# A graph network kernel on one core: round 0's gathered rows go through TensorE into PSUM before VectorE takes their maxima

## The chip, the cores and the metric

One Trainium2 chip, one of its cores. The metric is the time of one execution on the device in microseconds (us). The kernel before was run three times. Beside those runs stands one profiled execution, from which all rows here come.

## The reference, cut to what matters

There are 6250 nodes with 256 features each, and 100000 edges, sorted by their destination `dst`; `src` is random. All arithmetic is float32.

```python
# layer 0 (round 0 of the kernel)
theta_x = (x[dst] - x[src]) @ theta_w.T + theta_b
e = relu(theta_x + x[src] @ phi_w.T + phi_b)
x = layernorm(x + segment_max(e, dst))
# layer 1 (rounds 1 and 2)
hv = x @ W_in + b_in
for W, b in ((W_u0, b_u0), (W_u1, b_u1)):
    m = relu(concat([hv[src], edge_attr_64]) @ W + b)
    hv = where(has_in, segment_max(m, dst) + hv, hv)
x = layernorm(x + relu(hv @ W_ro + b_ro))
```

The part of an edge's message that hangs on the destination alone is the same for all edges of a run, so it can be added after the maximum. What is left per edge is a row of a table, picked by `src` (and in rounds 1 and 2 a product of the edge's 64 attributes).

## The kernel before, in words

Each of three rounds does the same four things. First a product over all nodes makes a table in HBM, `table0` to `table2` (49 tiles of 128 nodes, handled in 25 units of two). Then the edge pass goes over all edges. Its slots are laid out as 128 partitions of 784 steps, so a partition holds 784 edges in order of `dst`, and a step handles one edge of each partition. Then runs that cross from one partition to the next are joined, and at last the maxima are gathered back by node, which feeds the next round's products.

The edge pass is where most of the time lies. Its 784 steps are 49 turns of 16 steps (`BODY`). Four engines work on it side by side, each with its own written order, held together by semaphores:

- GpSimd (`gather_edges`, L518 to L527) issues one indirect DMA per step. It brings 128 rows of 256 floats from the table, by the indices in `src_sb`, into the ring `gath` of G = 36 slots in SBUF. Every second step it waits until the slot's old rows have been used.
- TensorE, in rounds 1 and 2 (`messages`, L732 to L749), sums two steps at a time in a PSUM bank of `edge_ps`: the product of the edge attributes (L744), then the gathered rows, multiplied by the identity (L746). Six banks are used in turn (`EDGE_BANKS`), so TensorE may be 12 steps ahead of VectorE.
- VectorE (`edge_maxima`, L342 to L366) makes one running maximum per step (L356): `hist[s] = max(hist[s-1] + lift[t], edges)`, where `lift` is very negative at the start of a run. In rounds 1 and 2 `edges` comes from PSUM; in round 0 it is the gathered row in SBUF itself, and VectorE waits for the gather's semaphore directly.
- SyncE stores each 8 steps of `hist` to `runs` in HBM (L472).

Round 0 has more to do beside this. For each turn there is a query: VectorE makes a one-hot matrix in the middle of the turn (`pick_rows`, L279 and L281), TensorE multiplies it by `dst_f` into `query_ps`, banks 4 and 5 of `edge_ps` (`pick`, L693), and after the turn VectorE counts in it where the runs of 128 nodes end (`find_ends`, L286 to L298). TensorE also makes one base product of a tile of nodes per turn (`back`, L685 and L687), which ScalarE copies out of `back_ps` (L595). Once, after turn 1, it multiplies the weights of layer 1 with one another (`multiply_weights`, L725 and L729). Its inputs need `bias_columns` on VectorE (L315). VectorE takes the results in `weights_and_biases` (L321 to L338) after turn 2. In round 0 TensorE's order is therefore: base products, query, weight products, turn by turn, with no matmul of edges among them (L769 to L774).

GpSimd in round 0 waits for `state_done`, which VectorE raises every two steps; in rounds 1 and 2 for `group_summed`, which TensorE raises every two steps (L521 to L524).

Of the kernel before, what the change touches and what calls it, by code (L numbers as in the profile page):

```python
# [5 lines left out]
P = 128  # L6
# [14 lines left out]
HE_CHUNKS = STEPS // HC  # L21
NHE = 4
BANKS = 4
EDGE_BANKS = 6
TILES = -(-NODES // P)
NPAD = TILES * P

# [6 lines left out]
XT_BUFS, ROW_BUFS, UNIT_BUFS = 12, 8, 4  # L34
CONV, NEXT0, NEXT1, OUT = range(4)
LATE_TURN = 1
FIRST_X_CHUNK = 20
assert TURNS == TILES and STEPS % SC == 0 and H % SC == 0 and G % GS == 0 and STEPS % HC == 0 and HC % GS == 0 and SC % GS == 0


def gnn_kernel(nc, a):
# [13 lines left out]
    with ctx:  # L55
# [76 lines left out]
        staged = lambda u: slots(hist, 2 * UNIT_BUFS, UNIT_BUFS, u)  # L132
        assert 2 * XT_BUFS <= G and 2 * (ROW_BUFS + UNIT_BUFS) <= G and 4 * UNIT_BUFS <= H

        edge_ps = ctx.enter_context(nc.psum_tensor("edge_ps", [P, EDGE_BANKS, 2 * D], f32))
        side_ps = ctx.enter_context(nc.psum_tensor("side_ps", [P, 2, 2 * D], f32))
        wide = lambda u: (unit(u)[1] - unit(u)[0]) * D
        product_ps = lambda u: edge_ps[:, u % BANKS, 0:wide(u)]
        turned_ps = lambda u: edge_ps[:, BANKS + u % 4, 0:wide(u)] if u % 4 < 2 else side_ps[:, u % 4 - 2, 0:wide(u)]
        query_ps = edge_ps[:, BANKS:BANKS + 2, :].rearrange("p b f -> p (b f)")  # L140
        back_ps = side_ps[:, 0, 0:D]
        join_ps = [edge_ps[:, BANKS + n, 0:D] for n in range(2)]

        cleared = sem("cleared")
# [90 lines left out]
        def _(dve):  # L235
# [81 lines left out]

            def weights_and_biases():
                dve.wait_ge(weights_mult, 1)
                for n, w in enumerate((w_in_n0, w_in_n1, w_in_ro)):  # L320
                    V.tensor_copy(flat(w[:, :, :]), edge_ps[:, n, :])  # L321
                for n, b_ps in ((NEXT0, edge_ps[:, 3, 0:D]), (NEXT1, edge_ps[:, 3, D:]), (OUT, side_ps[:, 1, 0:D])):
                    V.tensor_tensor(b_full[:, n, :], b_ps, rest[:, n, :], ALU.add)
                V.tensor_tensor(b_full[:, CONV, :], rest[:, CONV, :], b_add, ALU.add)
                after()
                V.tensor_copy(part[0], b_full)
                after()
                V.tensor_tensor(rest, b_full, part[0], ALU.subtract)
                after()
                V.tensor_copy(part[1], rest)  # L330
                after()
                V.tensor_tensor(rest, rest, part[1], ALU.subtract)
                after()
                V.tensor_copy(part[2], rest)
                V.tensor_scalar(b_parts[:, :, :], part[0], row_is[:, 0:1], None, ALU.mult)
                for m in (1, 2):
                    after()
                    last = V.scalar_tensor_tensor(b_parts[:, :, :], part[m], row_is[:, m:m + 1], b_parts[:, :, :],  # L338
                                                  ALU.mult, ALU.add)
                reached("all", last)  # L340

            def edge_maxima(r):  # L342
                for t in range(STEPS):
                    s = r * STEPS + t
                    if r == 0 and t % BODY == BODY // 2:
                        pick_rows(col_no[:, :])
                    if s % SC == 0 and s >= H:
                        dve.wait_ge(stored[s // SC % NS], 16 * (s // H))
                    if r == 0 and s % 2 == 0:
                        dve.wait_ge(gathered[s % G // 2], 2 * 16 * (s // G + 1))  # L350
                    elif r > 0 and s % GS == 0:
                        dve.wait_ge(group_summed, s // GS - GROUPS + 1)
                    V.drain()
                    bank, half = s // 2 % EDGE_BANKS, s % 2 * D
                    edges = gath[:, s % G, :] if r == 0 else edge_ps[:, bank, half:half + D]
                    state = V.scalar_tensor_tensor(hist[:, s % H, :], hist[:, (s - 1) % H, :], lift[:, t:t + 1], edges,  # L356
                                                   ALU.add, ALU.max)
                    if s % GS == GS - 1:
                        state.then_inc(state_done, 1)
                    if r == 0 and t % BODY == BODY - 1:  # L360
                        i = t // BODY
                        find_ends(i + 1, node_no[:, 0:1], end_row[:, i:i + 1], float(P))
                        if i == LATE_TURN:
                            bias_columns()
                        if i == LATE_TURN + 1:
                            weights_and_biases()  # L366

            def join_runs(r):
                dve.wait_ge(fix_turned, r + 1)
# [137 lines left out]
        def _(pool):  # L507
# [10 lines left out]
            def gather_edges(r):  # L518
                for t in range(STEPS):
                    s = r * STEPS + t  # L520
                    if s % GS == 0 and G <= s < STEPS + G:  # L521
                        pool.wait_ge(state_done, (s - G) // GS + 1)
                    elif s % GS == 0 and s >= G:
                        pool.wait_ge(group_summed, (s - G) // GS - GROUPS + 1)  # L524
                    pool.indirect_dma_start(gath[:, s % G, :], None, tables[r],  # L525
                                            bass.IndirectOffsetOnAxis(src_sb[:, t:t + 1], 0)
                                            ).then_inc(gathered[s % G // 2], 16)  # L527
# [41 lines left out]
        def _(act):  # L569
# [8 lines left out]
            def load_he(r, c):  # L578
                n = (r - 1) * HE_CHUNKS + c
                if n >= NHE:  # L580
                    act.wait_ge(group_summed, (n - NHE + 1) * HC // GS)
                act.dma_start(he_sb[:, n % NHE, :], a["he"][:, c * HC // 2 * P:(c + 1) * HC // 2 * P]
                              ).then_inc(he_loaded[n % NHE], 16)

# [94 lines left out]
        def _(pe):  # L679
# [39 lines left out]
            def multiply_weights():  # L719
                pe.wait_ge(setup_step, setup_at["b_in columns"])  # L720
                rights = (w_n0, w_n1, w_ro)
                for n, w in enumerate(rights):
                    for m in range(KH):
                        for h in range(KH):
                            T.matmul(edge_ps[:, n, m * D:(m + 1) * D], w_inT[:, h, m * P:(m + 1) * P], w[:, h, :],  # L725
                                     start=(h == 0), stop=(h == KH - 1))
                for w, to in zip(rights, (edge_ps[:, 3, 0:D], edge_ps[:, 3, D:], side_ps[:, 1, 0:D])):
                    for h in range(KH):
                        last = T.matmul(to, b_in_cols[:, h, :], w[:, h, :], start=(h == 0), stop=(h == KH - 1))  # L729
                last.then_inc(weights_mult, 1)  # L730

            def messages(r):  # L732
                for g in range(GROUPS):
                    n = (r - 1) * GROUPS + g
                    c = n * GS // HC
                    if n * GS % HC == 0:
                        pe.wait_ge(he_loaded[c % NHE], 16 * (c // NHE + 1))
                    if g * GS >= 2 * EDGE_BANKS:
                        pe.wait_ge(state_done, r * GROUPS + g - 2 * EDGE_BANKS // GS + 1)
                    for k in range(0, GS, 2):  # L740
                        s = r * STEPS + g * GS + k
                        bank = edge_ps[:, s // 2 % EDGE_BANKS, :]
                        at = s % HC // 2 * P
                        T.matmul(bank, he_sb[:, c % NHE, at:at + P], w_e[r - 1][:, :], start=True, stop=False)  # L744
                        pe.wait_ge(gathered[s % G // 2], 2 * 16 * (s // G + 1))
# [20 lines left out]

            for r in range(ROUNDS):
                if r == 0:
                    for i in range(TURNS):  # L769
                        for t in back_tiles(0, i):  # L770
                            back(t)
                        pick(i + 1)
                        if i == LATE_TURN:
                            multiply_weights()  # L774
                else:
                    pe.wait_ge(product_out, (r + 1) * NU)
                    messages(r)
# [62 lines left out]
```

## Time and profile before

| | us |
|---|---|
| median of three runs | 3344.41 (3342.88 to 3352.03) |
| the profiled execution's own time | 3344.26 |
| its span, first to last instruction | 3342.5 |

| engine | busy us | share of the span |
|---|---|---|
| TensorE matmul (PE) | 2113.1 | 63% |
| VectorE (DVE) | 1462.9 | 44% |
| ScalarE (ACT) | 188.2 | 6% |
| GpSimd (POOL) | 2412.3 | 72% |

The busy time of an engine is the sum of its instructions. It does not say what the engine waited for; the chain of waits and the groups of instructions by line do. Round 0's gathers start at 56.9 us, round 1's at 1190.5 us and round 2's at 2259.1 us. PE, PEld, DVE, ACT, POOL and SP are the profile's names of TensorE's matmul, its weight load, VectorE, ScalarE, GpSimd and SyncE. L12 is line 12 of the kernel. A float32 matmul shows as two records.

### The profile page before, as it was taken

Reading aid. Unit: us, or ns where it says so; the run is one execution under the profiler, and the core shown is the slowest. Engines: PE = TensorE matmul, PEld = TensorE weight load, DVE = VectorE, ACT = ScalarE, POOL = GpSimd, SP = SyncE. Lnnn points to the kernel's source line nnn. Section 1 sums busy time; section 2 is a strip of 40 time slices with the busy share of each in tenths; the row PEclk is TensorE's granted clock in tenths of the full one; section 3 lists DMA queues with packets and bytes.
Section 4 is the critical chain, followed back from the end, with each engine's and each line's share of the span. In section 5 each row is a group of like instructions: output and inputs, shape, how many; then the busy total and the mean of one; then the engine's idle time right before and its main releaser. Section 6 shows DMA issues by size and latency. Waiting matters only on the chain.

```text
span 3342.5 us, 21987 instructions
## 1 busy us (share of the span) xinstructions
PE 2113.1 (63%) x5442; PEld 1057.8 (32%) x5442; DVE 1462.9 (44%) x3430; ACT 188.2 (6%) x422; POOL 2412.3 (72%) x2536
## 2 busy tenths in 40 slices
PE   5322222222222678788888887877888888888877
PEld 4211111111111433333333333353443433333335
DVE  2655555555555523333433333423333333333337
ACT  1000000000000510000000000010000000000005
POOL 4777777777776457777777777757777777777766
PEclk8655555555555999999999999988999999999989
DMA  7666666666665557777777776776777777777765
GB/s 251 209 214 221 222 223 227 224 225 215 211 218 187 183 190 238 248 243 237 249 239 245 245 240 237 247 249 215 255 248 260 245 243 249 253 255 251 244 207 151
DMA packets 265662, 770.03 MB, mean 230 GB/s; under 512 B 55444, under 2 KB 114687, under 8 KB 227903
## 3 DMA queue, kind: packets, MB, share of 16 engines
q0 software_dynamic: 122208, 334.92, 32.9%
q1 hardware_dynamic: 84478, 354.64, 28.1%
q10 hardware_dynamic: 58848, 79.06, 8.0%
q8 instruction: 44, 0.72, 0.1%
q14 instruction: 84, 0.68, 0.1%
HBM read 421.22 MB, written 347.19 MB: 230 GB/s over the span
## 4 chain that ended last, share of the span: by engine, by line
POOL 46%; DMA 17%; issue 16%; PE 16%; DVE 3%; ACT 2%; DVEq 0%; ACTq 0%; POOLq 0%
POOL gath L525 45%; DMA gath<-table,src_sb 15%; PE edge_ps L746 6%; PE edge_ps L744 3%; PE edge_ps L685 3%; PE side_ps L685 2%; DVE hist L356 1%; POOL gath L552 1%; ACT x_sb L636 1%; DVE hist L393 1%; DMA gath<-runs,end_row 0%; ACT gath L636 0%; DMA runs<-hist 0%; PE edge_ps L757 0%; PE side_ps L757 0%
## 5 line engine op out<-in xcount | busy, mean ns | idle before, releaser
L525 POOL DMA_INDIRECT gath<-table,src_sb x2352 | 2244.7, 954 | 788.9 <-issue 670.3
L356 DVE SCALAR_TENSOR_TENSOR hist<-hist,lift,edge_ps 128x256 f32<-128x256 f32 x1568 | 752.6, 480 | 1231.4 <-PE edge_ps L746 1169.9
L746 PE MATMUL edge_ps<-gath,ident 128*128 128x512 f32 x1568 | 860.7, 632 | 335.7 <-DMA gath<-table,src_sb 334.8
L744 PE MATMUL edge_ps<-w_e,he_sb 128*128 128x512 f32 x1568 | 820.0, 605 | 1.0 <-DVE hist L416 0.5
L693 PE MATMUL edge_ps<-dst_f,onehot 128*128 128x512 f32 x200 | 145.9, 883 | 731.7 <-DVE onehot L281 731.7
L356 DVE SCALAR_TENSOR_TENSOR hist<-hist,lift,gath 128x256 f32<-128x256 f32 x784 | 380.9, 486 | 426.8 <-DMA gath<-table,src_sb 382.8
L746 PEld LDWEIGHTS edge_ps<-gath,ident 128*128 128x128 f32 x1568 | 288.2, 196 | 799.4 <-DMA gath<-table,src_sb 540.4
L744 PEld LDWEIGHTS edge_ps<-w_e,he_sb 128*128 128x128 f32 x1568 | 298.4, 196 | 351.0 <-issue 335.1
L693 PEld LDWEIGHTS edge_ps<-dst_f,onehot 128*128 128x128 f32 x200 | 57.8, 318 | 811.1 <-DVE onehot L281 760.5
L595 ACT COPY hv_sb<-side_ps 128x256 f32<-128x256 f32 x147 | 54.7, 372 | 2886.0 <-PE edge_ps L746 1867.5
L552 POOL DMA_INDIRECT gath<-runs,end_row x147 | 147.7, 1005 | 65.9 <-issue 40.2
L685 PE MATMUL side_ps<-w_theta,back_T 128*128 128x256 f32 x196 | 83.9, 575 | 21.0 <-DVE b_parts L338 19.3
L685 PEld LDWEIGHTS side_ps<-w_theta,back_T 128*128 128x128 f32 x196 | 60.6, 311 | 41.2 <-DVE b_parts L338 19.8
L685 PE MATMUL side_ps<-w_in_n,back_T 128*128 128x256 f32 x196 | 69.7, 493 | 0.0
L685 PE MATMUL side_ps<-w_in_ro,back_T 128*128 128x256 f32 x196 | 65.3, 467 | 0.0
L685 PEld LDWEIGHTS side_ps<-w_in_n,back_T 128*128 128x128 f32 x196 | 48.9, 249 | 36.4 <-issue 31.1
L685 PEld LDWEIGHTS side_ps<-w_in_ro,back_T 128*128 128x128 f32 x196 | 47.6, 243 | 37.1 <-issue 32.1
L685 PE MATMUL side_ps<-w_ro,back_T 128*128 128x256 f32 x196 | 58.2, 425 | 0.0
L685 PE MATMUL edge_ps<-w_ro,hist 128*128 128x256 f32 x196 | 50.4, 401 | 11.2 <-ACT hist L623 11.2
L289 DVE TENSOR_SCALAR_CACHE_REDUCE junk<-edge_ps,node_no 128x784 f32<-128x784 f32 x49 | 50.6, 1033 | 4.8 <-issue 0.4
L685 PE MATMUL edge_ps<-w_in_n,hist 128*128 128x256 f32 x196 | 50.7, 389 | 0.0
L286 DVE TENSOR_SCALAR_CACHE_REDUCE junk<-edge_ps,node_no 128x784 f32<-128x784 f32 x49 | 50.3, 1027 | 0.0
(125 smaller groups left out, 906.9 us busy)
## 6 DMA issues: line engine op xcount, KB each, us to landing
runs<-hist SPq DMA_DIRECT2D x294, 1024.0 KB, 5.2
he_sb<-in_he ACTq DMA_DIRECT2D x196, 256.0 KB, 2.9
gath<-table,src_sb POOLq DMA_INDIRECT x2352, 3.3
table<-hist SPq DMA_DIRECT2D x72, 256.0 KB, 2.8
back_T<-x1T ACTq DMA_DIRECT2D x98, 128.0 KB, 3.2
back_T<-in_xT ACTq DMA_DIRECT2D x49, 128.0 KB, 2.5
x_sb<-in_x SPq DMA_DIRECT2D x49, 128.0 KB, 4.8
back_T<-msgT ACTq DMA_DIRECT2D x49, 128.0 KB, 5.9
```

The lines of the kernel that those rows point to most:

```text
L286: V.tensor_scalar(junk[:, :], query_ps[:, 0:STEPS], nodes, 0.0, ALU.is_le, ALU.add, accum_out=counts[:, 0:1])
L289: V.tensor_scalar(junk[:, :], query_ps[:, 0:STEPS], nodes, 0.0, ALU.is_lt, ALU.add, accum_out=counts[:, 1:2])
L356: state = V.scalar_tensor_tensor(hist[:, s % H, :], hist[:, (s - 1) % H, :], lift[:, t:t + 1], edges, ALU.add, ALU.max)
L393: V.scalar_tensor_tensor(y, y, 0.0, flat(x_sb[:, lo:hi, :]), ALU.max, ALU.add)
L525: pool.indirect_dma_start(gath[:, s % G, :], None, tables[r], bass.IndirectOffsetOnAxis(src_sb[:, t:t + 1], 0)).then_inc(gathered[s % G // ...
L552: pool.indirect_dma_start(rows(u)[:, k, :], None, runs[0:SPARE, :], bass.IndirectOffsetOnAxis(end_row[:, lo + k:lo + k + 1], 0)).then_inc( ...
L595: A.copy(hv_sb[:, n % TILES, :], back_ps).then_inc(back_kept, 1)
L636: last = A.activation(to[:, k, :], of[:, k, :], ACT.Identity, bias=shift[:, at, k:k + 1], scale=rstd[:, at, k:k + 1])
L685: last = T.matmul(to, left, right, start=(m == 0), stop=(bias is None and m == len(terms) - 1))
L693: last = T.matmul(query_ps[:, lo:hi], onehot[:, :], dst_f[:, lo:hi], start=True, stop=True)
L744: T.matmul(bank, he_sb[:, c % NHE, at:at + P], w_e[r - 1][:, :], start=True, stop=False)
L746: last = T.matmul(bank, ident[:, :], flat(gath[:, s % G:s % G + 2, :]), start=False, stop=True)
```

## The change

In round 0 TensorE now multiplies each pair of gathered steps by the identity into a PSUM bank (`first_rows`), and VectorE's L356 takes `edges` from that bank, as in the other rounds. VectorE waits for `group_summed` in all rounds, and so does GpSimd. Round 0 uses three banks in turn, since banks 4 and 5 hold the query. The base products, the query and the weight products stand inside `first_rows`, between the pairs: base products after the third pair of a turn, the query for the turn after its seventh pair, the weight products after the second pair of turn 2. Their results go to banks 3 to 5 and the side banks instead of banks 0 to 3, and VectorE takes them at step 40, the middle of turn 2, ahead of that turn's `pick_rows`. The other edits follow the new counts of `group_summed`.

```diff
-EDGE_BANKS = 6
+EDGE_BANKS = (3, 6, 6)
+WEIGHTS_AT = (LATE_TURN + 1) * BODY + BODY // 2
...
+        weights_ps = [edge_ps[:, BANKS, :], edge_ps[:, BANKS + 1, :], side_ps[:, 0, :]]
+        edge_bank = lambda r, t: edge_ps[:, t // 2 % EDGE_BANKS[r], :]
...
             def edge_maxima(r):
                 for t in range(STEPS):
                     s = r * STEPS + t
+                    if r == 0 and t == WEIGHTS_AT:
+                        weights_and_biases()
                     if r == 0 and t % BODY == BODY // 2:
                         pick_rows(col_no[:, :])
...
-                    if r == 0 and s % 2 == 0:
-                        dve.wait_ge(gathered[s % G // 2], 2 * 16 * (s // G + 1))
-                    elif r > 0 and s % GS == 0:
-                        dve.wait_ge(group_summed, s // GS - GROUPS + 1)
+                    if s % GS == 0:
+                        dve.wait_ge(group_summed, s // GS + 1)
                     V.drain()
-                    bank, half = s // 2 % EDGE_BANKS, s % 2 * D
-                    edges = gath[:, s % G, :] if r == 0 else edge_ps[:, bank, half:half + D]
+                    edges = edge_bank(r, t)[:, t % 2 * D:(t % 2 + 1) * D]
...
-                    if s % GS == 0 and G <= s < STEPS + G:
-                        pool.wait_ge(state_done, (s - G) // GS + 1)
-                    elif s % GS == 0 and s >= G:
-                        pool.wait_ge(group_summed, (s - G) // GS - GROUPS + 1)
+                    if s % GS == 0 and s >= G:
+                        pool.wait_ge(group_summed, (s - G) // GS + 1)
...
+            def first_rows():
+                for g in range(GROUPS):
+                    turn_no, at = g // (BODY // GS), g % (BODY // GS) * GS
+                    if g == 0:
+                        pe.wait_ge(product_out, NU)
+                    if g * GS >= 2 * EDGE_BANKS[0]:
+                        pe.wait_ge(state_done, g - 2 * EDGE_BANKS[0] // GS + 1)
+                    for t in range(g * GS, (g + 1) * GS, 2):
+                        pe.wait_ge(gathered[t % G // 2], 2 * 16 * (t // G + 1))
+                        last = T.matmul(edge_bank(0, t), ident[:, :], flat(gath[:, t % G:t % G + 2, :]),
+                                        start=True, stop=True)
+                    last.then_inc(group_summed, 1)
+                    if turn_no == LATE_TURN + 1 and at == BODY // 8:
+                        multiply_weights()
+                    if at == BODY // 4:
+                        for t in back_tiles(0, turn_no):
+                            back(t)
+                    if at == BODY - 2 * GS:
+                        pick(turn_no + 1)
...
             for r in range(ROUNDS):
                 if r == 0:
-                    for i in range(TURNS):
-                        for t in back_tiles(0, i):
-                            back(t)
-                        pick(i + 1)
-                        if i == LATE_TURN:
-                            multiply_weights()
+                    first_rows()
```

## Rows read from the trace of the kernel before

**Rows 1.** Chain of waits: shares of the span by engine and line.

```profile
POOL gath L525 45%; DMA gath<-table,src_sb 15%; PE edge_ps L746 6%; PE edge_ps L744 3%; PE edge_ps L685 3%; PE side_ps L685 2%; DVE hist L356 1%; POOL gath L552 1%; ACT x_sb L636 1%; DVE hist L393 1%; DMA gath<-runs,end_row 0%; ACT gath L636 0%; DMA runs<-hist 0%; PE edge_ps L757 0%; PE side_ps L757 0%
```

**Rows 2.** Groups of instructions (count, busy us, mean ns, idle before): L525, rounds 0, 1.

```profile
L525 POOL DMA_INDIRECT gath<-table,src_sb x784 | 762.2, 972 | 261.9 <-issue 227.3 <-DMA table<-hist 23.3 <-DVE hist L356 11.3
...
L525 POOL DMA_INDIRECT gath<-table,src_sb x784 | 741.3, 946 | 278.0 <-issue 220.6 <-DMA table<-hist 39.4 <-PE edge_ps L746 16.8
```

**Rows 3.** Line L525: ns min/median/max, first and last start, rounds 0, 1, 2.

```profile
L525 POOL DMA_INDIRECT gath<-table,src_sb x784: 942/946/1761, 56.9 to 1056.7; - x196
...
L525 POOL DMA_INDIRECT gath<-table,src_sb x784: 942/946/962, 1190.5 to 2169.5; - x196
...
L525 POOL DMA_INDIRECT gath<-table,src_sb x784: 942/946/957, 2259.1 to 3237.8; - x196
```

**Rows 4.** Groups of instructions: L356 in round 0 and in round 1.

```profile
L356 DVE SCALAR_TENSOR_TENSOR hist<-hist,lift,gath 128x256 f32<-128x256 f32 x782 | 380.0, 486 | 425.6 <-DMA gath<-table,src_sb 381.6 <-issue 0.9
...
L356 DVE SCALAR_TENSOR_TENSOR hist<-hist,lift,edge_ps 128x256 f32<-128x256 f32 x778 | 373.5, 480 | 616.4 <-PE edge_ps L746 585.8 <-issue 1.7
```

**Rows 5.** Timeline (start us, duration us, instruction, idle before): gathers and VectorE, rounds 0, 1.

```profile
66.78 1.62 DVE L356 SCALAR_TENSOR_TENSOR hist<-hist,lift,gath 128x256 f32<-128x256 f32 x3 [8.89 <-DMA gath<-table,src_sb]
66.94 1.14 POOL L525 DMA_INDIRECT gath<-table,src_sb  x1 [0.30 <-issue]
...
127.73 1.23 DVE L328 TENSOR_TENSOR x_sb<-x_sb 128x1024 f32<-128x1024 f32 x1
128.19 1.66 POOL L525 DMA_INDIRECT gath<-table,src_sb  x1 [0.30 <-issue]
...
1052.90 1.04 POOL L525 DMA_INDIRECT gath<-table,src_sb  x1 [0.30 <-issue]
...
1204.90 1.04 DVE L356 SCALAR_TENSOR_TENSOR hist<-hist,lift,edge_ps 128x256 f32<-128x256 f32 x2 [1.66 <-PE edge_ps L746]
...
1205.50 0.95 POOL L525 DMA_INDIRECT gath<-table,src_sb  x1 [0.31 <-issue]
```

**Rows 6.** Busy by stretch (length, busy us of each engine, granted clock, DMA): in round 0.

```profile
690.00:890.00 200.00, 43.28 (x82) 23.98 (x83) 110.20 (x278) 3.52 (x10) 152.04 (x157) 0.54 0.66 215
```

**Rows 7.** Timeline: TensorE at the lower clock, rounds 0 and 1.

```profile
72.55 2.99 PE L693 MATMUL edge_ps<-dst_f,onehot 128*128 128x512 f32 x4 [18.63 <-DVE onehot L281]
...
157.12 1.91 PE L685 MATMUL side_ps<-w_theta,back_T 128*128 128x256 f32 x4
...
1194.52 2.07 PE L746 MATMUL edge_ps<-gath,ident 128*128 128x512 f32 x2 [6.00 <-DMA gath<-table,src_sb]
...
1198.09 1.91 PE L746 MATMUL edge_ps<-gath,ident 128*128 128x512 f32 x2
...
1199.80 1.45 PE L744 MATMUL edge_ps<-w_e,he_sb 128*128 128x512 f32 x2
```

**Rows 8.** Timeline: weight products, the query behind them, VectorE's block.

```profile
104.27 3.78 PE L725 MATMUL edge_ps<-x_sb 128*128 128x256 f32 x8 [10.00 <-DVE x_sb L315]
...
114.15 1.48 PE L693 MATMUL edge_ps<-dst_f,onehot 128*128 128x512 f32 x4
...
120.73 1.03 DVE L286 TENSOR_SCALAR_CACHE_REDUCE junk<-edge_ps,node_no 128x784 f32<-128x784 f32 x1
...
123.67 1.28 DVE L321 COPY w_in_n<-edge_ps 128x512 f32<-128x512 f32 x2
...
132.26 2.65 DVE L338 SCALAR_TENSOR_TENSOR b_parts<-x_sb,row_is,b_parts 128x1024 bf16<-128x1024 bf16 x2
```

**Rows 9.** Timeline: the end of the edge pass, rounds 0 and 1.

```profile
1056.74 0.95 POOL L525 DMA_INDIRECT gath<-table,src_sb  x1 [0.30 <-issue]
...
1059.52 1.04 DVE L356 SCALAR_TENSOR_TENSOR hist<-hist,lift,gath 128x256 f32<-128x256 f32 x2 [1.19 <-DMA gath<-table,src_sb]
...
2174.13 1.13 PE L746 MATMUL edge_ps<-gath,ident 128*128 128x512 f32 x2 [0.77 <-DMA gath<-table,src_sb]
...
2175.36 1.03 DVE L356 SCALAR_TENSOR_TENSOR hist<-hist,lift,edge_ps 128x256 f32<-128x256 f32 x2 [1.72 <-PE edge_ps L746]
```

More of the change, by code:

```diff
@@ L133, in gnn_kernel @@
         assert 2 * XT_BUFS <= G and 2 * (ROW_BUFS + UNIT_BUFS) <= G and 4 * UNIT_BUFS <= H
-        edge_ps = ctx.enter_context(nc.psum_tensor("edge_ps", [P, EDGE_BANKS, 2 * D], f32))
+        edge_ps = ctx.enter_context(nc.psum_tensor("edge_ps", [P, max(EDGE_BANKS), 2 * D], f32))
         side_ps = ctx.enter_context(nc.psum_tensor("side_ps", [P, 2, 2 * D], f32))
@@ L319, in weights_and_biases @@
                 dve.wait_ge(weights_mult, 1)
-                for n, w in enumerate((w_in_n0, w_in_n1, w_in_ro)):
-                    V.tensor_copy(flat(w[:, :, :]), edge_ps[:, n, :])
+                for w, w_ps in zip((w_in_n0, w_in_n1, w_in_ro), weights_ps):
+                    V.tensor_copy(flat(w[:, :, :]), w_ps)
                 for n, b_ps in ((NEXT0, edge_ps[:, 3, 0:D]), (NEXT1, edge_ps[:, 3, D:]), (OUT, side_ps[:, 1, 0:D])):
@@ L364, in edge_maxima @@
                             bias_columns()
-                        if i == LATE_TURN + 1:
-                            weights_and_biases()
             def join_runs(r):
@@ L580, in load_he @@
                 if n >= NHE:
-                    act.wait_ge(group_summed, (n - NHE + 1) * HC // GS)
+                    act.wait_ge(group_summed, GROUPS + (n - NHE + 1) * HC // GS)
                 act.dma_start(he_sb[:, n % NHE, :], a["he"][:, c * HC // 2 * P:(c + 1) * HC // 2 * P]
@@ L724, in multiply_weights @@
                         for h in range(KH):
-                            T.matmul(edge_ps[:, n, m * D:(m + 1) * D], w_inT[:, h, m * P:(m + 1) * P], w[:, h, :],
+                            T.matmul(weights_ps[n][:, m * D:(m + 1) * D], w_inT[:, h, m * P:(m + 1) * P], w[:, h, :],
                                      start=(h == 0), stop=(h == KH - 1))
@@ L737, in messages @@
                         pe.wait_ge(he_loaded[c % NHE], 16 * (c // NHE + 1))
[L738 to L742, printed above, removed]
+                    if g * GS >= 2 * EDGE_BANKS[r]:
+                        pe.wait_ge(state_done, r * GROUPS + g - 2 * EDGE_BANKS[r] // GS + 1)
+                    for t in range(g * GS, (g + 1) * GS, 2):
+                        s = r * STEPS + t
+                        bank = edge_bank(r, t)
                         at = s % HC // 2 * P
```

## The prediction, made before the changed kernel ran

> **What bounds the kernel now.** I read the chain of waits first. The gather that GpSimd issues, L525, has 45% of it alone, and its transfers another 15% [rows 1]. Then I read the groups of instructions, one round at a time [rows 2]. In each round GpSimd issues 784 gathers. Between two of them it stands 0.30 us of "issue"; nothing else holds it inside a round: the 11.3 us put down to VectorE in round 0 are 37 of those same 0.30 us steps, and the 23.3 us are the wait for the table before the first gather. So each round lasts 784 times (one gather plus 0.30), whatever TensorE and VectorE do, as long as they keep up. They do: VectorE is idle 425.6 us in round 0, nearly all of it waiting for gathered rows [rows 4], and TensorE is busy 43 us of 200 [rows 6].
>
> The reader should see one oddity. The same gather takes 972 ns on average in round 0 and 946 ns in round 1 [rows 2], with a longest of 1761 against 962 ns [rows 3]. From first to last start, round 0 needs 1056.7 - 56.9 = 999.8 us and round 1 needs 2169.5 - 1190.5 = 979.0 us [rows 3]: 20.8 us more for the same 784 gathers (busy alone: 762.2 - 741.3 = 20.9 [rows 2]).
>
> **Where the 20.9 us come from.** I went to the timeline of round 0. 143 of 784 gathers take over 0.97 us; the first that meets an L356 starts at 66.94, the last at 1052.90 [rows 5]. Their pattern is sharp. At 66.78 VectorE begins an L356; at 0.48 us each it ends at 67.26. At 66.94 a gather starts, and takes 1.14 us instead of 0.95, so 0.19 longer. 67.26 is 0.32 after its start. Going through all of them, a gather is stretched when a VectorE instruction with two SBUF tensors as inputs is already running and lasts beyond about 0.14 us after the gather's start; the stretch is what it lasts beyond that (0.32 - 0.14 = 0.18). The longest fits too: L328, two SBUF inputs, runs from 127.73 to 128.96; the gather of 128.19 takes 1.66, so 0.71 more, and 128.96 - (128.19 + 0.14) = 0.63 [rows 5]. In round 1 L356 takes one input from PSUM, and still meets gathers: from 1204.90 a pair of L356 runs for 1.04 us, to 1205.94, and the gather that starts under the second of them, at 1205.50, takes 0.95 [rows 5]. No gather of rounds 1 and 2 takes more than 962 ns [rows 3]. So it is the second SBUF input, not VectorE's writes or its being busy. Going by which instruction lay over each gather's start, L356 carries 18.6 us of the 20.9, L328 and L332 together 1.5, and the small ones (L281's two-input comparison above all) and noise the rest.
>
> The Trainium skill (SBUF — State Buffer, on engine ports and the shared port pair) says a VectorE instruction with two SBUF inputs contends with a GpSimd instruction that reads SBUF, and that the later one waits until the other ends; the trace agrees, since the stretch ends with the VectorE instruction, and a gather reads its indices from SBUF. The same page infers that a two-input operation takes only the read interface while descriptor generation needs the write interface, which would leave a DMA issue untouched. By that sentence the gain of this change would be nil (a rival below); the 143 stretched gathers speak against it here.
>
> **The change part by part**, against the profiled execution's 3344.3 us (span 3342.5, and 1.8 around it); the median of the three runs is 3344.4, so the sums carry over.
>
> (1) Round 0's L356 reads its edge operand from PSUM. It becomes the L356 of rounds 1 and 2, 480 ns for 486 [rows 4]; VectorE's own time doesn't count, it is hidden by its 425.6 us of idling. What counts is the 18.6 us of stretched gathers: -18.6. Bounds: -20.9 if all stretch goes, 0 if round 1's lack of stretch had another reason. I take -18.6, as rounds 1 and 2 show the new form with none.
>
> (2) TensorE gets 392 new identity matmuls of 128x512, two gathered rows each. Each shows as two records; such a pair takes 2.07 us at the lower clock when it comes after a pause, and 1.71 from start to start when work follows work (1198.09 to 1199.80) [rows 7]. Per turn of 16 gathers (20.0 us of GpSimd): 8 x 1.71 = 13.7, a query 2.99, a base product 1.91, together 18.6 us even at the lower clock [rows 7]; at the higher one about half (a query 1.48 [rows 8], an identity pair 1.13 alone [rows 9]). That fits into 20.0, and the gather ring holds 36 rows, 45 us. Cost while it fits: 0. If it did not: the rival below.
>
> (3) Queries now wait in TensorE's order behind the matmul of steps 12 and 13 of a turn, and VectorE asks at step 8, so the query is ready when TensorE comes to it; VectorE needs the answer after step 15. TensorE's 2.99 us fall between two pairs due 2.5 us apart, so VectorE may run 1 to 2 us late at a turn's end and make it up: it needs 16 x 0.56 (a pair 1.04 less one 0.48 [rows 5]) and the search for run ends, 2.9 us (120.73 to 123.67 [rows 8]), of a turn's 20. GpSimd is now released by TensorE, not VectorE, and never has been close to the release. Cost 0; bounds 0 to 1 us, at the last turn alone.
>
> (4) The weight products (TensorE from 104.27 to 114.15 us) now stand ahead of round 0's matmuls, and VectorE's block that takes them (123.67 to 134.9) starts at step 40 instead of after 47 [rows 8]. While they run, TensorE sums nothing: it holds at step 36 for 10 us, then gets at most three pairs ahead of VectorE and holds at step 46 while VectorE works its 11 us block. At about 130 us GpSimd has issued (130 - 57)/1.25 = 58 gathers and may issue 46 + 36 = 82: 24 gathers, 30 us, are left. VectorE recovers 5 us per turn. Cost 0; if the ring didn't cover it, at most 10 + 11 = 21 us. L328 and L332 stay, with two SBUF inputs, and can again meet two gathers (1.5 us, kept in the sum) or none. The base products are two per turn in turns 3 to 5, 1.9 us each more, also inside the reserve.
>
> (5) Edge banks 3 instead of 6 in round 0: TensorE is at most 6 steps ahead, 7.5 us of gathers, against VectorE's 2.9 us search at a turn's end. Cost 0. The counts in GpSimd's and ScalarE's waits only follow the new numbering; rounds 1 and 2 wait for the same events: 0.
>
> (6) The end of round 0. Now the last gather starts at 1056.74 and VectorE takes its rows at 1059.52, 2.8 us later [rows 9]. A matmul comes between landing and VectorE: in round 1 it starts at 2174.13 and VectorE follows at 2175.36, 1.2 us [rows 9]; at the lower clock 2.07 and the 0.1 us step to VectorE, 2.2 [rows 7]. All of it is on the path. I take +1.7, between the two, because TensorE's clock in this stretch may be either. The queries' chain at the end keeps its distance. At the start of round 0 TensorE is free before the first rows land: 0.
>
> Sum: -18.6 + 1.7 = -16.9; 3344.3 - 16.9 = 3327.4, about 3327 us. Own range: gathers -20.9 to -16 (L281 and the rest may meet more gathers once L356 no longer pushes them), end +1.2 to +2.2 with 2 us either way for how long the last transfers take to land: 3321 to 3333.
>
> **Rivals.**
> (a) The stretch does not go, 6%. Either the gathers are held by VectorE for a reason that PSUM doesn't mend, or TensorE's new reads of the gather ring replace it. Against it: TensorE reads the same ring in rounds 1 and 2 with 946 ns gathers. Then 3344.3 + 1.7 = 3346. (The inference of the Trainium skill's page SBUF — State Buffer, told above, would give this number too.)
> (b) TensorE becomes the bound in round 0 and the kernel is slower, 5%. Its place: each pair released singly at the lower clock, so that 2.07 counts each time instead of 1.71: 8 x 2.07 + 2.99 + 1.91 = 21.5 us per turn against 20.0. From turn 3 on that is 46 x 1.5 = 69 us; the ring hides the 30 us that (4) leaves of it, and the rest, 39, shows: 3327 + 39 = 3366. It decides from 20.0 us per turn on. For it: the granted clock is 0.54 in round 0 [rows 6]. Against it: a late TensorE has its pairs waiting, and then 1.71 holds; and in round 1 the clock rose after 6 us of such work: the pair of 1199.80 takes 1.45 [rows 7].
> (c) Partial: the remaining two-input instructions fall into step with the gathers, or the weight phase costs some of its 21 us, so that 8 to 12 us of the gain go: 3337, 7%.
>
> **How the numbers follow.** Forecast 82%, (a) 6%, (b) 5%, (c) 7%. Range 3321 to 3337: the forecast's own, widened to (c). A change under 0.3%, 10 us, can't be told from none here. Faster (under 3334): 0.87, the forecast and a part of (c); same 0.08; slower 0.05, (b) alone.
>
> **What would show it.** Right: the gathers of round 0 average 946 to 950 ns, and some 980 us lie between first and last start; longest ones only at L328, L332; VectorE released by TensorE; GpSimd idle in steps of 0.30 only; VectorE's last pair some 4.5 us after the last gather's start instead of 2.8. Wrong: gathers still at 972 ns (a); idle of GpSimd released by TensorE in round 0, longer than 0.3 each (b, or the weight phase in c).

## The result, and the profile after

Over eight runs the changed kernel takes 3334.39 us (3332.28 to 3338.73), the kernel before 3344.20 us in as many. The medians lie 9.8 us apart. The ratio is 0.9966 with a 95% interval of 0.9958 to 0.9975, which is 8 to 14 us faster. The prediction said 3327, in a range from 3321 to 3337. The profiled execution took 3333.97 us with a span of 3332.2.

The gather is L523 now and the maximum L358. The chain of waits of the changed kernel still has the gather at its head, with 41% instead of 45% [rows 1]:

```profile
POOL gath L523 41%; DMA gath<-table,src_sb 17%; PE edge_ps L764 6%; PE edge_ps L683 3%; PE edge_ps L739 3%; PE edge_ps L762 3%; PE side_ps L683 3%; POOL gath L550 1%; ACT x_sb L634 1%; PE edge_ps L691 1%; DMA gath<-runs,end_row 1%; DVE hist L393 1%; ACT gath L634 0%; DMA runs<-hist 0%; PE side_ps L775 0%
```

The groups of instructions of round 0 in the changed kernel (count, busy us, mean ns, idle before), gather and maximum:

```profile
L523 POOL DMA_INDIRECT gath<-table,src_sb x784 | 743.1, 948 | 261.5 <-issue 227.6 <-DMA table<-hist 23.0 <-PE edge_ps L739 11.0
...
L358 DVE SCALAR_TENSOR_TENSOR hist<-hist,lift,edge_ps 128x256 f32<-128x256 f32 x782 | 375.3, 480 | 414.6 <-PE edge_ps L739 363.6 <-issue 0.9
```

and the gather's line: ns min/median/max, first and last start in round 0:

```profile
L523 POOL DMA_INDIRECT gath<-table,src_sb x784: 942/946/1763, 56.6 to 1037.3; - x196
```

The gather is down from 972 to 948 ns [rows 2], and first and last start lie 980.7 us apart instead of 999.8 [rows 3]. The 11.0 us that name TensorE are 36 steps of 0.30: GpSimd never waited for a free slot. VectorE is idle 415 us around its maxima, about as long as before [rows 4], now behind TensorE.

Cutting the two spans at GpSimd's instructions gives the whole account (us; "fix" is the read of rows to fix, GpSimd's first instruction after a round's gathers):

| stretch | before | after | difference |
|---|---|---|---|
| to round 0's first gather | 56.9 | 56.6 | -0.3 |
| round 0, first to last gather | 999.9 | 980.7 | -19.1 |
| round 0, last gather to fix | 8.5 | 15.6 | +7.1 |
| fix to round 1's first gather | 125.2 | 125.9 | +0.6 |
| round 1, first to last gather | 979.0 | 978.6 | -0.4 |
| to round 2's first gather | 89.7 | 91.3 | +1.6 |
| round 2, first to last gather | 978.7 | 978.9 | +0.2 |
| to the end | 104.7 | 104.7 | 0.0 |

The gain is there in full, and 7.1 us are given back in a single place, the end of round 0. This is its timeline in the changed kernel:

```profile
1030.14 2.46 ACTq L580 DMA_DIRECT2D he_sb<-in_he  x4
...
1035.21 0.32 SPq L472 DMA_DIRECT2D runs<-hist  x1
...
1037.28 0.95 POOL L523 DMA_INDIRECT gath<-table,src_sb  x1 [0.30 <-issue]
1037.82 2.04 PE L739 MATMUL edge_ps<-gath,ident 128*128 128x512 f32 x2 [0.91 <-DMA gath<-table,src_sb]
...
1040.89 2.04 PE L739 MATMUL edge_ps<-gath,ident 128*128 128x512 f32 x2 [1.03 <-DMA gath<-table,src_sb]
1042.73 2.83 PE L691 MATMUL edge_ps<-dst_f,onehot 128*128 128x512 f32 x4
...
1045.35 1.73 PE L739 MATMUL edge_ps<-gath,ident 128*128 128x512 f32 x2
1047.18 1.04 DVE L358 SCALAR_TENSOR_TENSOR hist<-hist,lift,edge_ps 128x256 f32<-128x256 f32 x2 [3.10 <-PE edge_ps L739]
...
1052.91 0.94 POOL L532 DMA_INDIRECT fix_rows<-runs,fix_from  x1 [14.69 <-DMA runs<-hist]
```

VectorE takes the last pair 9.9 us after the last gather's start, against 2.8 [rows 9]. Two things can be seen. The pair before the last is still waiting for its rows (the releaser is the DMA) 3.6 us after the last gather has started. Then the last turn's query takes 2.6 us ahead of the last pair. The last two pairs of matmuls take 2.04 and 1.73 us, where c0 below has 1.10 for the same work; the granted clock just before them is 0.50 (second view below). There is also something that the prediction did not have: four loads of edge attributes for round 1 (`he_sb`), 256 KB each, 7.1 us before the last gather. In the kernel before they start 20.4 us before it:

```profile
1036.33 1.79 ACTq L582 DMA_DIRECT2D he_sb<-in_he  x4
```

ScalarE issues them after it has copied out the last base product, and that product moved from turn 47 into turn 48. The store of eight steps of maxima that lies nearest to the last gather moved too: it started 6.2 us before it and starts 2.1 us before it now, since VectorE gets to those steps later. The stretches around the last gather (length, busy of each engine, and at the end clock, DMA share, GB/s), before and then after, show what this does: the DMA engines are full where they used to have room.

```profile
1048.70:1052.70 4.00, 1.31 (x2) 0.80 (x3) 2.66 (x8) 0.00 (x0) 2.98 (x4) 0.50 0.59 210
1052.70:1056.70 4.00, 1.68 (x3) 0.38 (x2) 0.96 (x3) 0.00 (x0) 2.92 (x3) 0.50 0.84 262
```

```profile
1029.30:1033.30 4.00, 1.70 (x7) 0.65 (x5) 3.42 (x13) 1.04 (x2) 2.96 (x4) 0.98 0.93 281
1033.30:1037.30 4.00, 2.49 (x3) 0.50 (x2) 2.65 (x7) 0.62 (x1) 2.90 (x4) 0.50 1.06 395
```

### The profile page after: what moved, and what is told of

Read it like the earlier page. It is cut to its first block, busy times and chain, and to the rows that moved or that the text cites. A ratio compares the mean times of both kernels' runs of the same rounds, so it can differ in the third digit from the quotient of the medians.

```text
span 3332.2 us, 23945 instructions
## 1 busy us (share of the span) xinstructions
PE 2514.5 (75%) x6226; PEld 1198.1 (36%) x6226; DVE 1459.7 (44%) x3430; ACT 188.4 (6%) x422; POOL 2394.7 (72%) x2536
## 4 chain that ended last, share of the span: by engine, by line
POOL 43%; PE 19%; DMA 19%; issue 15%; ACT 2%; DVE 2%; DVEq 0%; ACTq 0%; POOLq 0%
POOL gath L523 41%; DMA gath<-table,src_sb 17%; PE edge_ps L764 6%; PE edge_ps L683 3%; PE edge_ps L739 3%; PE edge_ps L762 3%; PE side_ps L683 3%; POOL gath L550 1%; ACT x_sb L634 1%; PE edge_ps L691 1%; DMA gath<-runs,end_row 1%; DVE hist L393 1%; ACT gath L634 0%; DMA runs<-hist 0%; PE side_ps L775 0%
## 5 line engine op out<-in xcount | busy, mean ns | idle before, releaser
L523 POOL DMA_INDIRECT gath<-table,src_sb x2352 | 2225.4, 946 | 789.7 <-issue 667.8
L358 DVE SCALAR_TENSOR_TENSOR hist<-hist,lift,edge_ps 128x256 f32<-128x256 f32 x2352 | 1129.0, 480 | 1649.0 <-PE edge_ps L764 1169.7
L764 PE MATMUL edge_ps<-gath,ident 128*128 128x512 f32 x1568 | 856.4, 629 | 333.3 <-DMA gath<-table,src_sb 332.5
L739 PE MATMUL edge_ps<-gath,ident 128*128 128x512 f32 x784 | 483.1, 732 | 342.2 <-DMA gath<-table,src_sb 324.6
L764 PEld LDWEIGHTS edge_ps<-gath,ident 128*128 128x128 f32 x1568 | 288.6, 195 | 792.8 <-DMA gath<-table,src_sb 530.7
L739 PEld LDWEIGHTS edge_ps<-gath,ident 128*128 128x128 f32 x784 | 155.2, 228 | 599.0 <-issue 341.9
L691 PE MATMUL edge_ps<-dst_f,onehot 128*128 128x512 f32 x200 | 93.7, 600 | 11.1 <-DVE onehot L284 11.1
L691 PEld LDWEIGHTS edge_ps<-dst_f,onehot 128*128 128x128 f32 x200 | 47.0, 236 | 76.3 <-issue 63.2
L683 PE MATMUL side_ps<-w_theta,back_T 128*128 128x256 f32 x196 | 72.8, 511 | 1.7 <-ACT hv_sb L593 1.7
L683 PEld LDWEIGHTS side_ps<-w_theta,back_T 128*128 128x128 f32 x196 | 52.6, 270 | 45.2 <-issue 39.3
L292 DVE TENSOR_SCALAR_CACHE_REDUCE junk<-edge_ps,node_no 128x784 f32<-128x784 f32 x49 | 50.6, 1033 | 4.8 <-issue 0.4
```

The lines of the kernel that those rows point to most:

```text
L292: V.tensor_scalar(junk[:, :], query_ps[:, 0:STEPS], nodes, 0.0, ALU.is_lt, ALU.add, accum_out=counts[:, 1:2])
L683: last = T.matmul(to, left, right, start=(m == 0), stop=(bias is None and m == len(terms) - 1))
L691: last = T.matmul(query_ps[:, lo:hi], onehot[:, :], dst_f[:, lo:hi], start=True, stop=True)
L739: last = T.matmul(edge_bank(0, t), ident[:, :], flat(gath[:, t % G:t % G + 2, :]), start=True, stop=True)
L764: last = T.matmul(bank, ident[:, :], flat(gath[:, s % G:s % G + 2, :]), start=False, stop=True)
```

## The experiments

Two questions were open: whether the second SBUF input alone makes the 19 us, and what costs 7 us at the end of round 0. The runs of each table row were compared with runs of the kernel before on the same chip. "Stream" is first to last gather of round 0, "end" is last gather to fix.

| kernel | stream | end | ratio to before (95%) |
|---|---|---|---|
| before | 999.9 | 8.5 | |
| after | 980.7 | 15.6 | 0.9966 (0.9958 to 0.9975) |
| c0_changed_again | 981.6 | 13.1 | 0.9966 (0.9952 to 0.9979) |
| e1_sbuf_max | 1003.6 | 14.5 | 1.0024 (1.0014 to 1.0033) |
| e2_stale_psum | 981.4 | 8.5 | 0.9950 (0.9936 to 0.9963) |
| e5_one_input | 992.2 | 8.3 | 0.9971 (0.9959 to 0.9982) |
| e3_query_early | 981.6 | 14.5 | 0.9966 (0.9954 to 0.9978) |
| e4_direct_tail | 981.8 | 12.1 | 0.9962 (0.9948 to 0.9975) |
| e8b_all_three | 984.1 | 9.0 | 0.9951 (0.9938 to 0.9965) |
| e9b_before_late_loads | 999.9 | 10.2 | 1.0002 (0.9993 to 1.0011) |

Stream and end are of one profile each. The last two rows ran on a chip where the unstretched gathers of rounds 1 and 2 need 981 us instead of 979, so their streams are some 2 us longer for that alone.

### Is it the second SBUF input?

**e1_sbuf_max** takes back one line of the change: VectorE reads the gathered row in SBUF again. GpSimd then has to wait for VectorE too before it reuses a slot; that wait was never felt, since no step between two gathers of round 0 is over 0.32 us.

```diff
-                    edges = edge_bank(r, t)[:, t % 2 * D:(t % 2 + 1) * D]
+                    edges = gath[:, s % G, :] if r == 0 else edge_bank(r, t)[:, t % 2 * D:(t % 2 + 1) * D]
...
+                    if s % GS == 0 and G <= s < STEPS + G:
+                        pool.wait_ge(state_done, (s - G) // GS + 1)
```

> The changed kernel, but in round 0 VectorE reads the gathered row in SBUF again; TensorE still passes every pair to PSUM, and VectorE waits for it as in the changed kernel. Theory S (the second SBUF input alone stretches the gathers): gathers of round 0 back from 948 to about 972 ns, time 3334.4 + 18.6 = 3353, slower than the kernel before, because the end of round 0 keeps its price. Rival O (order, TensorE's work or clock bring the gain): 948 ns, 3334.

Measured: 3355.13 us against 3346.73 on that chip, and round 0's gathers:

```profile
L525 POOL DMA_INDIRECT gath<-table,src_sb x784 | 765.9, 977 | 261.6 <-issue 209.3 <-DMA table<-hist 23.0 <-PE edge_ps L741 15.5
```

The stretch is back, 977 ns, with TensorE's matmuls, VectorE's waits and the order all as in the changed kernel. The kernel is slower than before, because it pays the end (14.5 us) and gains nothing. Its stream is 3.7 us longer than before's, for the same instruction: 159 gathers take over 0.97 us here and 147 there. How many are hit, and for how long, hangs on where the maxima fall against the gathers.

**e2_stale_psum** is the opposite: the kernel before, with only the place of the operand changed.

```diff
-                    edges = gath[:, s % G, :] if r == 0 else edge_ps[:, bank, half:half + D]
+                    edges = gath[:, s % G, :] if s < 3 * BODY else edge_ps[:, 0, 0:D] if r == 0 else edge_ps[:, bank, half:half + D]
```

> The kernel before, in which round 0's L356 takes its second input from step 48 on from a PSUM bank that nobody rewrites (so round 0's maxima are left out from there); no matmul is added, the order of TensorE, the waits and the end of the round are before's. Theory S (the second SBUF input alone stretches the gathers): gathers of round 0 from 972 to about 948 ns, 736/784 x 18.6 = 17.5 us less, 3344.2 - 17.5 = 3326.7, and a step of 8.5 us at the end: the gain without its price. Rival O (TensorE's new work, its clock or the waits bring the gain): 972 ns, 3344.

Measured: 3327.82 us against 3345.21. The gathers of its round 0:

```profile
L525 POOL DMA_INDIRECT gath<-table,src_sb x784 | 743.8, 949 | 261.7 <-issue 227.9 <-DMA table<-hist 23.2 <-DVE hist L356 10.7
```

This is 949 ns without one added matmul, and the end stays at 8.5 us. Together the two runs show that the operand's place makes the 19 us, and that TensorE's part only pays. One rival is left by them: that it is the reading of the `gath` ring, into which the gathers write, and not the second input. The profile of the kernel before speaks against it. L328 and L332 subtract tensors in `x_sb` and do not touch the ring, and the gathers that met them took 1.66 and 1.76 us.

**e5_one_input** asks whether it must be two SBUF inputs.

```diff
-                    state = V.scalar_tensor_tensor(hist[:, s % H, :], hist[:, (s - 1) % H, :], lift[:, t:t + 1], edges,
-                                                   ALU.add, ALU.max)
+                    if r == 0:
+                        state = V.tensor_scalar(hist[:, s % H, :], edges, lift[:, t:t + 1], None, ALU.max)
...
```

> The kernel before, in which round 0's maximum is a tensor_scalar with a single SBUF tensor as input, the gathered row (the running maximum is left out in round 0); everything from and to SBUF. Theory S in its narrow form (two SBUF inputs are needed): no gather of round 0 over 0.97 us but the handful of the weight block, 3344.2 - 18.6 = 3325.6. The rival is that page SBUF — State Buffer of the Trainium skill is right on two-port modes: a float32 tensor_scalar from SBUF to SBUF holds the shared ports as well, and gathers are still stretched where one lies over their start; the instruction is shorter (about 0.3 us by L279's 0.28 for 128 elements), so 5 to 15 us of stretch are left, 3331 to 3341.

Measured: 3337.79 us against 3346.73, gathers of 963 ns. The narrow form of theory S fell: with a single SBUF input 111 gathers of round 0 still take over 0.97 us, though none longer than 1.1 outside the weight block, and some 13 us of stretch are left. The rival had said 5 to 15 us and 3331 to 3341. The timeline shows one such gather, and the VectorE pair that met it:

```profile
208.85 0.78 DVE L357 TENSOR_SCALAR hist<-gath,lift 128x256 f32<-128x256 f32 x2 [0.59 <-DMA gath<-table,src_sb]
...
211.45 0.98 DVE L357 TENSOR_SCALAR hist<-gath,lift 128x256 f32<-128x256 f32 x2 [1.82 <-DMA gath<-table,src_sb]
212.19 1.06 POOL L528 DMA_INDIRECT gath<-table,src_sb  x1 [0.31 <-issue]
```

Gather and VectorE each lose: 0.11 us on the one, 0.20 on the pair. The page SBUF — State Buffer of the Trainium skill (who interferes with whom) says this of copies and tensor_scalar in a two-port mode; the trace agrees that a one-input float32 operation from SBUF to SBUF contends, but here it doesn't show in which mode it ran. VectorE is held at another place here than with two inputs. Of the 163 L357 that start 0.45 to 0.70 us after a gather's start, 132 are lengthened, the longest to 0.60 us from 0.35; of the 149 L356 of the kernel before that start there, none takes over 0.486 us. What can be said beyond that is that a maximum with one input in SBUF and one in PSUM stretches no gather: in e2's 736 such steps, in the changed kernel, and in rounds 1 and 2.

### What costs 7 us at the end of round 0?

**c0_changed_again** is the changed kernel, unedited.

> The changed kernel once more, for a second profile of the end of round 0 on the chip that also runs the next three. In its first profile the read of rows to fix starts 15.6 us after round 0's last gather starts (8.5 before). Theory T (the query of the last turn stands before the last pair and is on the path): again 13 to 16 us. Rival L (the pair of steps 780 and 781 happened to land late, 6.2 us after its gather started): some 10 to 11 us in this profile, and the time scatters by the difference. Time by both: 3334.

It took 3332.00 us against 3345.21. Its end of round 0:

```profile
1036.86 0.95 POOL L523 DMA_INDIRECT gath<-table,src_sb  x1 [0.30 <-issue]
1039.61 1.10 PE L739 MATMUL edge_ps<-gath,ident 128*128 128x512 f32 x2 [3.23 <-DMA gath<-table,src_sb]
1040.54 1.48 PE L691 MATMUL edge_ps<-dst_f,onehot 128*128 128x512 f32 x4
...
1043.06 1.10 PE L739 MATMUL edge_ps<-gath,ident 128*128 128x512 f32 x2 [1.04 <-DMA gath<-table,src_sb]
1044.27 1.04 DVE L358 SCALAR_TENSOR_TENSOR hist<-hist,lift,edge_ps 128x256 f32<-128x256 f32 x2 [2.42 <-PE edge_ps L739]
```

Here the query is over before the last rows are there: the last pair waits for the DMA until 6.2 us after its gather's start, where 2.8 us were enough in the kernel before. So the query was not the whole cause, and late rows were no accident of one profile. In e1's profile, too, the last rows landed 6.3 us after their gather's start.

**e3_query_early** moves the query: `if at == BODY - 2 * GS:` becomes `if at == BODY // 2:`.

> The changed kernel with the query behind the pair of steps 8 and 9 of a turn instead of 12 and 13; nothing else. Theory T: the last turn's query is done long before the last rows land, so 2.6 us of query and the cold pair that waits behind it go: the step from last gather to the read of rows to fix falls from 15.6 to about 10.5 us, time 3334.4 - 4 = 3330. Rival L: the step scatters as before, time 3334. Gathers of round 0 stay at 948 ns.

It took 3334.14 us, the same ratio as the changed kernel, and its last rows came later still:

```profile
1038.40 0.95 POOL L523 DMA_INDIRECT gath<-table,src_sb  x1 [0.30 <-issue]
...
1045.01 2.04 PE L739 MATMUL edge_ps<-gath,ident 128*128 128x512 f32 x2 [0.61 <-DMA gath<-table,src_sb]
1047.16 1.04 DVE L358 SCALAR_TENSOR_TENSOR hist<-hist,lift,edge_ps 128x256 f32<-128x256 f32 x2 [1.62 <-PE edge_ps L739]
```

Theory T falls as the cause of the 7 us; in the first profile the query had its 2.6. Here it is out of the way, and nothing is won, because the rows by themselves land only 6.5 us after their gather's start, against 2.7 in the kernel before.

**e4_direct_tail** adds to e3 that VectorE reads the last four steps from SBUF.

```diff
+                    direct = r == 0 and t >= STEPS - DIRECT
+                    if s % GS == 0 and direct:
+                        dve.wait_ge(gathered[s % G // 2], 2 * 16 * (s // G + 1))
...
+                    edges = gath[:, s % G, :] if direct else edge_bank(r, t)[:, t % 2 * D:(t % 2 + 1) * D]
```

> As e3_query_early, and the last 4 steps of round 0 are read by VectorE from SBUF as in the kernel before (TensorE still passes them, unused). If the matmul between landing and VectorE is the rest of the cost at the end, the step from last gather to the read of rows to fix falls to before's 8.5 us: another 1.2 to 2.2 us, time 3328. If what is left is late landing, it equals e3_query_early.

It took 3331.46 us; its end is 12.1 us, not 8.5. VectorE now waits for the rows directly, and starts on the last two pairs 5.3 us after the last gather's start:

```profile
1038.15 0.95 POOL L527 DMA_INDIRECT gath<-table,src_sb  x1 [0.30 <-issue]
...
1043.42 2.18 DVE L362 SCALAR_TENSOR_TENSOR hist<-hist,lift,gath 128x256 f32<-128x256 f32 x4 [2.75 <-DMA gath<-table,src_sb]
```

What is left is landing. In this kernel the four loads start 4.0 us before the last gather, and a store of eight steps of maxima (1 MB) 2.0 us before it. That led to theory H: the loads that moved delay the last rows. The edit issues them in mid-round:

```diff
                 for i in range(TURNS):
...
+                    if r == 0 and i == TURNS // 2:
+                        first_he(1)
...
             feed_edges(0)
-            first_he(1)
```

**e6_loads_mid, e7_query_loads, e8_all_three, e9_before_late_loads** put this into the changed kernel, into e3, into e4, and its opposite into the kernel before (`act.wait_ge(state_done, GROUPS - 4)` ahead of `first_he(1)`).

> The changed kernel, with the four loads of edge attributes for round 1 (256 KB each) issued by ScalarE in the middle of round 0 instead of after its last base product. In the kernel before they start 20.4 us before the last gather; in the changed one 7.1 and 3.8 us before it, and the last rows land late. Theory H (the loads, together with a 1 MB store of maxima, delay the last gathers): rows land some 3 us after their gather again; left are the matmul and the query in front of the last pair, so the step from last gather to the read of rows to fix is 10.5 (upper clock) to 12.3 us (lower), mean of before and changed kernel; time 3334.4 - 3 = 3331. Rival T (the query alone): still 13 to 16 us, 3334. Rival L (chance in landing): scatter from 11 to 16.

> The early query and the loads in mid-round together. Theory H: neither late rows nor a query before the last pair, only the matmul is left: 8.5 + 1.2 to 2.2 = 9.7 to 10.7 us, time 3334.4 - 4.5 = 3330. Rival L: as e3_query_early, 12 to 15 us.

> Early query, loads in mid-round, and the last 4 steps read from SBUF without a matmul between. Theory H: before's step of 8.5 us, so the whole gain of the gathers stays: time as e2_stale_psum or 3344.5 - 18.5 = 3326, the best correct kernel. Rival L: 12 us as in e4_direct_tail, 3331.

> The kernel before, with the same four loads held back until step 775 of round 0 is done, which is some 6 us before the last gather starts. Nothing else changes. Theory H: the last rows land late as in the changed kernel, the step from last gather to the read of rows to fix grows from 8.5 to 11 to 13 us, time 3345 + 3.5 = 3348.5. Rivals T and L: 8.5 us, 3345.

These four can't answer the question, and none of their expected times was met. They ran on a chip where the kernel before takes 3845.70 us, and the fix of e6 starts 31.9 us after the last gather (1173.07 to 1204.96). The ratios there are 0.9978 (0.9963 to 0.9994), 1.0044 (1.0027 to 1.0061), 1.0041 (1.0025 to 1.0057) and 0.9999 (0.9982 to 1.0017). Why the two with the early query, e7 and e8, are slower than the kernel before there is open. The last two of the four were run again on another chip.

> e8_all_three again: its first runs were on a chip where every kernel, the one before too, needs 15% longer and rows land tens of us late, so they say nothing on 3 us. It differs from e4_direct_tail (12.1 us from round 0's last gather to the read of rows to fix, 3331.5) by one edit, the four loads in mid-round. Theory H (these loads and a 1 MB store delay the last gathers): 8.5 to 9.5 us, time 3345 - 18.5 = 3327, like e2_stale_psum. Rival L (chance in landing): some 12 us, 3331.

It took 3336.77 us against 3351.64. Its end of round 0:

```profile
1040.77 0.95 POOL L527 DMA_INDIRECT gath<-table,src_sb  x1 [0.30 <-issue]
...
1042.95 2.18 DVE L362 SCALAR_TENSOR_TENSOR hist<-hist,lift,gath 128x256 f32<-128x256 f32 x4 [0.92 <-DMA gath<-table,src_sb]
...
1049.81 0.95 POOL L536 DMA_INDIRECT fix_rows<-runs,fix_from  x1 [8.09 <-DMA runs<-hist]
```

VectorE starts on the last two pairs 2.2 us after the last gather's start instead of 5.3. The kernel differs from e4 by this one edit; the two profiles are of different chips. The end is 9.0 us. The ratio, 0.9951, is that of e2_stale_psum, the change without its price. It is the fastest kernel here that computes the reference; its interval still overlaps the changed kernel's, so the 4 to 7 us less at the end are seen in the profiles and not shown in the times.

> e9_before_late_loads again, for the same reason: the kernel before with only the four loads held back until step 775 of round 0 is done. Theory H: from 8.5 to 11 to 13 us, time 3 to 4 us over the kernel before. Rivals T and L: 8.5 us, the time of before.

It took 3352.85 us against 3351.64. The end grew from 8.5 to 10.2 us, half of what H wanted and not nothing, as T and L wanted; the time did not move measurably. So late loads cost the kernel before some 1.7 us in this profile. The landing of the last rows, after their gather's start, narrows down the rest. It is 2.7 us in the kernel before. With late loads and the store where it was (e9b) it is 4.2. With the late store and no late loads (e8b, the store from 3.3 us before the last gather to 1.3 after it) it is 3.1. With both it is 4.1 in the changed kernel's first profile and 6.1 to 6.5 in c0, e1, e3 and e4. So the loads do more than the store, and together they go with more than either alone. With one profile of each that is likely and not shown.

## Why the prediction was right, and which term was off

- **The bound and its stretch, right.** The step "a gather is stretched when a VectorE instruction with two SBUF tensors as inputs is already running" was sized at -18.6 us; the stream lost 19.1, 18.3 in the second profile and 18.5 in e2. What is left is where it was said: 18 gathers over 0.97 us, the longest, 1763 ns, under the weight block's subtraction. "So it is the second SBUF input" was too narrow (e5), but right for L356.
- **The rule of the stretch, incomplete.** "Already running" is not enough. In the kernel before, all 126 gathers that an L356 overlapped from 0.099 us or more before their start were stretched (counting L356 that lasted 0.17 us or more beyond the gather's start). None of the 72 was stretched over which the L356 began less than 0.098 us before. There the L356 itself is lengthened, to 0.55 us at most, and ends 0.46 us after the gather's start; e1 shows the same split (133 and 83). Here is one in the kernel before, a pair of 1.11 us instead of 1.04 over a gather of normal length:

```profile
599.09 1.11 DVE L356 SCALAR_TENSOR_TENSOR hist<-hist,lift,gath 128x256 f32<-128x256 f32 x2 [2.28 <-DMA gath<-table,src_sb]
599.18 0.95 POOL L525 DMA_INDIRECT gath<-table,src_sb  x1 [0.30 <-issue]
```

No L356 that starts 0 to 0.9 us after a gather's start, 537 of them, takes over 0.487 us. So the recorded "the later one waits until the other ends" and "the trace agrees" hold for the gather, and not for VectorE. The size of the term came from measured stretches and did not suffer.
- **TensorE's added work (2) at no cost, right; rival (b) did not come.** TensorE is busy 134 us of 200 (43 before [rows 6]), 13.4 us of a turn's 20.0, at a granted clock of 0.81 instead of 0.54, the same stretch as there. The claim that it fits "even at the lower clock", 18.6 us of 20.0, was therefore not put to the test:

```profile
690.00:890.00 200.00, 134.41 (x257) 56.17 (x257) 109.77 (x280) 3.95 (x11) 151.25 (x161) 0.81 0.67 221
```

- **The weight block (4), right.** TensorE's products take from 105.33 to 113.21 us, VectorE's block follows at 116.42, TensorE waits 11.1 us for the next query, and GpSimd shows not one step above 0.32 us between its gathers.
- **The inference that a descriptor-generating DMA isn't held by a two-input operation, wrong here:** e1 and e2 differ from their base by the operand's place, and by 22.9 and 18.5 us of stream. Which part of the gather is held, the reading of its indices or the writing of its descriptors, no run here shows.
- **The end of round 0 (6), mis-sized.** It was put at +1.7, the matmul between landing and VectorE, with VectorE's last pair some 4.5 us after the last gather's start. It measured +7.1 and +4.6 in two profiles, with that pair at 9.9 and 7.4 us. Part (3) allowed the query "0 to 1 us, at the last turn alone"; in the first profile it was 2.6. And the sentence "2 us either way for how long the last transfers take to land" treated as chance what the change itself does: the base product of the last turn moved 13 us later, and with it the four loads that ScalarE issues behind it. They fell on the last gathers, and the last rows landed 4.1 to 6.5 us after their gather's start in the five profiles of c0, e1, e3, e4 and the changed kernel, against 2.7 before. With e8b's three edits the end is 0.5 us from before's.
- Forecast and profile differ by 16.9 - 10.3 = 6.6 us. The end makes 5.4 of it; the rest is +0.6 and +1.6 in transitions that the change doesn't touch, less 1.0 in the gathers and the start. The same transitions scatter by some 3 and 5 us among the kernels of the table.
- **In part luck.** 3334.39 lies outside the forecast's own range, 3321 to 3333, and inside the stated one only by what (c) added to it. What (c) named, two-input instructions falling into step with the gathers or a price of the weight phase, did not happen; the end of the round took the 5 us instead. "Faster (under 3334)", held at 0.87, was missed by 0.4 us, although the interval of the ratio shows the kernel faster. The count of 143 gathers over 0.97 us is 147 in the trace.

## What to carry to other kernels

Where GpSimd issues DMAs without a pause, look at the spread of its instruction durations, not at their median, and lay the long ones against VectorE's timeline: moving one VectorE operand to PSUM gave 19 us of round 0's stream here, of which 10 were left in the kernel's time, although neither VectorE nor PSUM was a bottleneck. When a step moves in one engine's order, follow every engine that waits for it to what that engine does next: the loads behind ScalarE's copy were in no line of the diff. And a step that serves only the steady state (the matmul, the query) can be left out for the last few iterations, where its latency is on the path.

## What the runs showed of the hardware that was not expected

- A VectorE tensor_scalar with one float32 SBUF input of 128x256 contends with GpSimd's gathers too, and is itself lengthened: a pair takes 0.98 us where others take 0.78, gathers 1.06 where others take 0.95 (e5).
- Against a maximum with two SBUF inputs a gather is held only if the maximum began 0.1 us or more before it (kernel before and e1), and is then longer by what the maximum lasts beyond some 0.13 us after the gather's start. If the maximum began less than 0.1 us before it, the gather stays at 0.95 us and VectorE loses up to 0.07 us.
- One chip ran the five kernels that were timed on it 15% slower (3845.70 us for the kernel before). e6's gathers still took 950 ns each in round 0, as the changed kernel's do elsewhere, but the stream grew to 1116.7 us, with pauses of up to 7.7 us between two gathers. The order of the kernels changed there: e8, 0.5% faster than the kernel before on another chip, was 0.4% slower.
